# Pairwise message layer and attention: the tail of a batch element rebuilt and moved

## The reference

```python
# layer 0: a message for each pair (i, j)
hi = x @ W1[:H];  hj = x @ W1[H:]
h  = relu(hi[:, :, None, :] + hj[:, None, :, :] + b1)
y  = layernorm(h @ W2 + b2) * gamma + beta       # over the features, for every pair
o  = einsum('bij,bijh->bih', adj, y)
x1 = _layernorm(x + o)
# layer 1: attention
Wh = x1 @ W_w.T + W_b
s  = (Wh @ a_w[:C])[:, :, None] + (Wh @ a_w[C:])[:, None, :] + a_b
e  = exp(s) * adj;  alpha = e / e.sum(axis=2)
out = _layernorm(x1 + alpha @ x1)
```

## Time and profile before

| | |
|---|---|
| median of 3 runs | 2623.7 us (2622.17 to 2623.79) |
| profiled execution, span | 2621.4 us |
| TensorE busy | 2577.0 us, 98% |
| TensorE weight loads | 2049.5 us, 78% |
| VectorE busy | 2337.8 us, 89% |
| ScalarE busy | 2332.6 us, 89% |
| GpSimd busy | 1999.1 us, 76% |
| chain that ended last | PE 58%, DVE 24%, issue 11%, ACT 6% |

### The profile page before, as it was taken

How to read it: one execution, slowest core, us unless ns; L and a number is a source line. 1 busy time by engine, 2 the same in 40 slices (tenths; PEclk the granted TensorE clock), 3 DMA queues, 4 the chain that set the end, 5 groups by cost and what they waited for, 6 DMA issues and landing times.

```text
span 2621.4 us, 77145 instructions
## 1 busy us (share of the span) xinstructions
PE 2577.0 (98%) x21263; PEld 2049.5 (78%) x21263; DVE 2337.8 (89%) x18135; ACT 2332.6 (89%) x3650; POOL 1999.1 (76%) x1163
## 2 busy tenths in 40 slices
PE   8999999999999999999999999999999999999997
PEld 7777777777777777777777777777777777777774
DVE  7889988989899889998898989988988999989897
ACT  7899899899998998989989889999899898998996
POOL 7777777777777777777777777777777777777773
PEclk9999999999999999999999999999999999999999
DMA  0000000000000000000000000000000000000000
GB/s 17 8 12 7 11 7 10 11 6 11 11 6 11 6 11 11 6 11 11 6 11 6 11 11 6 11 10 7 11 6 11 11 6 11 8 8 11 6 7 7
DMA packets 48051, 23.49 MB, mean 9 GB/s; under 512 B 6208, under 2 KB 47808, under 8 KB 47808
## 3 DMA queue, kind: packets, MB, share of 16 engines
q1 hardware_dynamic: 46512, 21.12, 2.9%
q10 hardware_dynamic: 1296, 0.20, 0.0%
HBM read 17.11 MB, written 4.19 MB: 8 GB/s over the span
## 4 chain that ended last, share of the span: by engine, by line
PE 58%; DVE 24%; issue 11%; ACT 6%; POOL 0%; ACTq 0%; DVEq 0%; DMA 0%
PE y_ps L529 42%; DVE squares L517 16%; PE agg_ps L573 12%; DVE q L517 3%; ACT y L263 3%; DVE x1e L488 2%; ACT h L281 1%; ACT L334 1%; PE prep_ps L529 1%; PE tail_ps L529 1%; DVE o_sb L455 1%; PE tail_ps L584 1%; PE att_ps L529 1%; DVE eT L509 0%; DVE si_cols L499 0%
## 5 line engine op out<-in xcount | busy, mean ns | idle before, releaser
L252 POOL TENSOR_TENSOR h<-bT,aT 128x1024 f32<-128x1024 f32 x1024 | 1951.1, 1919 | 584.3 <-PE y_ps L529 572.9
L529 PEld LDWEIGHTS y_ps<-w_pair,h 128*128 128x128 f32 x16384 | 1885.7, 192 | 313.0 <-DVE q L517 260.3
L529 PE MATMUL y_ps<-w_pair,h 128*128 128x128 f32 x16384 | 1991.3, 278 | 21.9 <-DVE q L517 9.3
L517 DVE CUSTOM_DVE_ANT_0 squares<-y_ps,y 128x128 bf16<-128x128 f32 x8192 | 1842.3, 282 | 185.0 <-ACT y L263 171.2
L263 ACT ACTIVATE y<-y_ps 128x508 f32<-128x508 f32 x2048 | 1162.4, 595 | 190.8 <-PE y_ps L529 173.9
L281 ACT ACTIVATE h<-h 128x1024 f32<-128x1024 f32 x1024 | 1085.3, 1060 | 10.2 <-POOL h L252 10.2
L517 DVE DVE_READ_ACCUMULATOR2_ANT q<- 128x1 f32 x8192 | 659.1, 80 | 0.0
L573 PE MATMUL agg_ps<-y,wz 128*32 128x512 f32 x4096 | 545.9, 606 | 1.7 <-DVE o_sb L455 1.7
L573 PEld LDWEIGHTS agg_ps<-y,wz 128*32 128x32 f32 x4096 | 81.1, 108 | 66.7 <-issue 3.1
L492 DVE CUSTOM_DVE_ANT_0 s_terms<-x1e,v1row 128x128 f32<-128x128 f32 x64 | 99.5, 1554 | 0.1
L334 ACT ACT_TABLE_LOAD x64 | 82.1, 1283 | 4.3 <-DVE sj L504 3.2
(11 more groups left out here) (90 smaller groups left out, 740.4 us busy)
## 6 DMA issues: line engine op xcount, KB each, us to landing
x_in<-in_x_dram SPq DMA_DIRECT2D x64, 64.0 KB, 1.8
adj_in<-in_adj_dram SPq DMA_DIRECT2D x64, 64.0 KB, 1.9
x_res<-in_x_dram SPq DMA_DIRECT2D x64, 64.0 KB, 1.8
adj_res<-in_adj_dram SPq DMA_DIRECT2D x64, 64.0 KB, 1.9
out_dram<-x_out SPq DMA_DIRECT2D x64, 64.0 KB, 1.6
w<-in_L_gnn_W_dram ACTq DMA_DIRECT2D x1, 64.0 KB, 2.4
w1a<-in_L_gnn_W_dram SPq DMA_DIRECT2D x1, 64.0 KB, 2.2
w1b<-in_L_gnn_W_dram SPq DMA_DIRECT2D x1, 64.0 KB, 2.3
```

What stands on the lines that cost most here:

```text
L252: nc.gpsimd.tensor_tensor(h[:, u % HRING].rearrange("k (r g) s -> k r g s", g=GROUPS), bT[:, p, :].unsqueeze(1).unsqueeze(1).broadcast_to( ...
L517: last = nc.vector.tensor_tensor_reduce(out=squares[:, k % YRING, n, :], in0=y_ps[k % YRING][:, n, :], in1=y[:, p, i, :], scale=1.0, scala ...
L529: return nc.tensor.matmul(dst, lhsT, rhs, start=start, stop=stop)
```

## The change

- `x1p`, `ex` and `x2p` now lie in the PSUM bank of `att_ps`, `v` in that of `tail_ps`. They were in SBUF.
- rstd and the two layernorm factors are exp(-0.5 ln(var + eps)), both steps on ScalarE, with one table set loaded at the start. Before it was Sqrt on ScalarE and a reciprocal on VectorE, and tables were changed twice a slot.
- The score sums read `x1p` with the factor as their scale, and the rows v1row and v2row are made free of their mean in the set-up. `si_cols` is made by ScalarE, and the residual plus beta by ScalarE (`beta_part`) and GpSimd (`x_beta`, at its unit 7).
- Tail and finish of an element are in one slot, each step one unit behind the one that it needs: o_sb in VectorE's unit 1, its transpose before TensorE's unit 2, oT copy in ScalarE's unit 3, w_back before unit 4, x1p in unit 5, Ln and Exp in 6, x1e and the score sums in 7, si_cols in 8, scores before 9, ex in 10, eT in 11, attention before 12, x2p in 13, Ln and Exp in 14, x_out in 15.
- The eight groups of sums of an element come in four bursts of two, behind units 6, 9, 12 and 15 of one slot.
- `pair_weights` is at GpSimd's unit 5, `prep` a unit earlier on each engine. ScalarE's Ln and Exp of `v` stand in unit 0, ahead of the copy of quart 0 and behind the relu of unit 2. The last slot of the program falls away.

The diff, cut to its core:

```diff
-    WEIGHTS_UNIT = 4
-    POOL_WEIGHTS_UNIT = 8
-    CHUNK_STEP = UNITS // CHUNKS
-    EARLY_CHUNKS = (UNITS - WEIGHTS_UNIT) // CHUNK_STEP
+    POOL_WEIGHTS_UNIT, POOL_RESIDUAL_UNIT = 5, 7
+    BURST = {u: range(c, c + 2) for u, c in ((6, 0), (9, 2), (12, 4), (15, 6))}
...
+        v = tail_ps[:, 2, :]
+        x1p = ex = att_ps[:, 2 * K:3 * K]
+        x2p = att_ps[:, 3 * K:4 * K]
...
             # GpSimd
+                    if tail and u == POOL_RESIDUAL_UNIT:
+                        pool.wait_ge(beta_part_ready, t - 1)
+                        pool.wait_ge(xres_loaded[p], nth16(half, p, -2) * 2)
+                        nc.gpsimd.tensor_tensor(x_beta[:], beta_part[:], x_res[:, p, :], ALU.add).then_inc(x_beta_ready, 1)
...
             # ScalarE, behind the relu of unit u + 2 and ahead of the copies of unit u
+            nc.scalar.preload_act_table_set("natural_log_exp_and_others")
...
-                    if gather and u == 2:
-                        act.wait_ge(v_ready, t)
-                        nc.scalar.activation(sd[:], v[:], ACT.Sqrt, bias=epsc[:, 0:1], scale=1.0 / K).then_inc(sd_ready, 1)
+                    if gather and u == 0:
+                        act.wait_ge(v_ready, t)
+                        nc.scalar.activation(ln_v[:], v, ACT.Ln, bias=epsc[:, 0:1], scale=1.0 / K).then_inc(ln_v_ready, 1)
+                        act.wait_ge(ln_v_ready, t)
...
+                        nc.scalar.activation(rstd[:], ln_v[:], ACT.Exp, scale=-0.5).then_inc(rstd_ready, 1)
+                    if tail and u == 2:
+                        act.wait_ge(adj_sum_ready, t - 1)
...
+                        nc.scalar.activation(beta_part[:], beta_rows[:], ACT.Identity, scale=adj_sum[:, 0:1]).then_inc(beta_part_ready, 1)
+                    if tail and u == 3:
+                        act.wait_ge(oT_ps_s, t - 1)
...
+                        copy(oT_sb[:], tail_ps[:, 0, :]).then_inc(oT_sb_s, 1)
+                    if tail and u == 6:
+                        act.wait_ge(mv1_ready, t - 1)
+                        nc.scalar.activation(ln1[:], mv1[:, 1:2], ACT.Ln, bias=epsc[:, 0:1]).then_inc(ln1_ready, 1)
...
+                    if tail and u == 14:
+                        act.wait_ge(mv2_ready, t - 1)
+                        nc.scalar.activation(ln2[:], mv2[:, 1:2], ACT.Ln, bias=epsc[:, 0:1]).then_inc(ln2_ready, 1)
+                        act.wait_ge(ln2_ready, t - 1)
+                        nc.scalar.activation(rs2[:], ln2[:], ACT.Exp, scale=-0.5).then_inc(rs2_ready, 1)
...
             # VectorE
-                    if gather and (u, e) == (2, 0):
-                        nc.vector.reciprocal(rstd[:], sd[:]).then_inc(rstd_ready, 1)
-                    if tail and (u, e) == (3, 0):
+                    if tail and (u, e) == (0, 1):
+                        dve.wait_ge(xres_loaded[p], nth16(half, p, -2) * 2)
...
+                        nc.vector.reduce_sum(adj_sum[:], adj_res[:, p, :], axis=mybir.AxisListType.X).then_inc(adj_sum_ready, 1)
+                    if tail and (u, e) == (1, 0):
                         dve.wait_ge(agg_done, (t - 1) * CHUNKS)
                         nc.vector.tensor_scalar(o_sb[:], agg_ps[:, 0:K], part[:, 0:1], None, ALU.mult).then_inc(o_part, 1)
-                    if tail and u == 3 and 1 <= e < CHUNK:
+                    if tail and u == 1 and 1 <= e < CHUNK:
...
+                    if tail and (u, e) == (7, 1):
+                        nc.vector.tensor_tensor_reduce(out=s_terms[:, 1, :], in0=x1p, in1=v1row[:], scale=rs1[:, 0:1], scalar=0.0,
+                                                       op0=ALU.mult, op1=ALU.add, accum_out=si[:, 0:1]).then_inc(si_ready, 1)
...
+                    if tail and (u, e) == (15, 0):
+                        dve.wait_ge(rs2_ready, t - 1)
...
             # TensorE
-                    if finish and u == 0:
-                        pe.wait_ge(eT_ready, t - 2)
-                        mm(att_ps[:, 0:K + 1], eT[:], x1e[:]).then_inc(att_done, 1)
-                    if tail and u == 6:
+                    if tail and u == 2:
                         pe.wait_ge(o_stored, t - 1)
+                        if gather:
+                            pe.wait_ge(ln_v_ready, t)
                         nc.tensor.transpose(tail_ps[:, 0, :], o_sb[:], ident[:]).then_inc(oT_ps_s, 1)
-                    if tail and u == 8:
+                    if tail and u == 4:
                         pe.wait_ge(oT_sb_s, t - 1)
                         mm(tail_ps[:, 1, :], oT_sb[:], w_back[:]).then_inc(f_ps_s, 1)
...
+                    if tail and u == 12:
+                        pe.wait_ge(eT_ready, t - 1)
+                        pe.wait_ge(x1_ready, t - 1)
+                        mm(att_ps[:, 0:K + 1], eT[:], x1e[:]).then_inc(att_done, 1)
...
+                    if gather and u in BURST:
+                        for chunk in BURST[u]:
...
+                            weighted_sums(1 - p, chunk)
```

More of the change, by code:

```diff
@@ L107, in gnn_pair_kernel @@
         q = sb("q", [S, 2, S])
-        v, sd = sb("v", [S, S]), sb("sd", [S, S])
+        ln_v = sb("ln_v", [S, S])
         rstd = sb("rstd", [S, S])
@@ L176, in _, with slot @@
                     sp.dma_start(b1c[:], b1.rearrange("(p o) -> p o", o=1)).then_inc(s_w1, 16)
-            def slot(t, half, p, pairs, prep, gather, tail, finish, early):
+            def slot(t, half, p, pairs, prep, gather, tail, early):
                 if pairs and not (isinstance(t, int) and t + 2 >= B):
@@ new lines, in slot @@
+                    if tail and (u, e) == (13, 1):
+                        dve.wait_ge(rz_ready, t - 1)
+                        dve.wait_ge(x1_ready, t - 1)
+                        nc.vector.scalar_tensor_tensor(out=x2p, in0=att_ps[:, 0:K], scalar=rz[:, 0:1], in1=x1e[:, 0:K],
+                                                       op0=ALU.mult, op1=ALU.add).then_inc(x2p_ready, 1)
+                    if tail and (u, e) == (13, 2):
+                        dve.wait_ge(x2p_ready, t - 1)
+                        nc.vector.bn_stats(st2[:], x2p).then_inc(st2_ready, 1)
@@ new lines, in slot @@
+                    if tail and (u, e) == (13, 3):
+                        dve.wait_ge(st2_ready, t - 1)
+                        dve.sem_inc(s_passed, 1)
+                        nc.vector.bn_aggr(mv2[:], st2[:]).then_inc(mv2_ready, 1)
+                    if tail and (u, e) == (15, 0):
+                        dve.wait_ge(rs2_ready, t - 1)
+                        if early >= 3:
+                            dve.wait_ge(stored[1 - p], nth16(half, p, -3))
+                        nc.vector.tensor_scalar(x_out[:], x2p, mv2[:, 0:1], rs2[:, 0:1], ALU.subtract, ALU.mult).then_inc(out_ready, 1)
```

203 lines of the change are left out of this document (76 added, 127 removed).

## The result

The changed kernel takes 2879.8 us (median of 4 runs, 2876.3 to 2883.9) against 2623.1 (2622.2 to 2623.8) of the kernel before, both timed on the same chip: ratio 1.098, 95% interval 1.096 to 1.100. Slower, by 257 us; 2880 had been forecast. The profiled execution spans 2874.2 us (before 2621.4).

The account below looks back on a forecast made before the run. TensorE, busy 98% of 2621.4 us, was taken as the bound. Per slot 40.34 - 0.9 - 1.35 + 3.5 + 0.45 + 1.6 = 43.65; 62 slots add 205, back edges 53, drain -3, median 2.3: say 2880 us, range 2700 to 2960.

Parts of the forecast that it names:

- the PEclk row: Sign expected in the profile after: granted clock below 1.0 behind the wait, and this row showing 8 and 9.
- The added wait: TensorE, at the transpose of o_sb before unit 2, waits for VectorE's last o_sb: 3.5 us a slot taken.
- the walk: Step-by-step timing of TensorE, ScalarE and VectorE from the end of unit 15's matmuls (T) to the last o_sb: wait 3.7 us.
- Rival B: At the transpose ScalarE is prompt, wait 2.6 us, half the back edge hides: 2796 us, about 2700 without clock fall; chance 0.13.
- rival C: Wait at the transpose is at its 1.6 us floor, clock holds, back edges hide: 2593 us; chance 0.05.
- The back edge: At each of 28 loop turns VectorE is held before v; counted whole, 1.9 us each, 53 us in all.
- The other short links: TensorE waits for oT_sb before unit 4 (about 0.2 us) and eT before unit 12 (0.25): +0.45 a slot.
- own work of 38.1: TensorE's work per slot without waits, said to fall from 39.4 to 38.1 us with sums in bursts.
- The clock: TensorE's granted clock falls after the wait at the transpose: 1.6 us charged per slot, bounds 0 and 2.5.
- Rival A: The wait at the transpose is as computed but TensorE's clock holds: 2780 us; chance 0.17.
- saving of -1.35: On TensorE, the second group of a burst costs 0.86 us, not 1.20: -0.34, four times a slot.
- TensorE's 0.9 us of waits: TensorE's waits per slot in the kernel before, all granted as returned by the relief of VectorE and ScalarE: -0.9.

Follow-up runs that it names:

- experiment 1: Changed kernel with TensorE's transpose of o_sb before unit 3 instead of unit 2: 2681.2 us, ratio 1.022.
- Experiment 5: Changed kernel with ScalarE's Ln and Exp of v in unit 2, not 0, and GpSimd's scaled weights one unit later: 2793.1 us, ratio 1.065.
- experiment 11: Changed kernel with tail spread out, Ln and Exp of v in unit 2, bursts behind units 1, 6, 10, 13, o_sb in VectorE's unit 2: 2542.3 us.
- experiment 2: Changed kernel with 14 useless products on TensorE ahead of its wait for o_sb: 2831.1 us, ratio 1.080.
- experiment 7: Changed kernel with about two units between each tail step and its consumer, and Ln and Exp of v in ScalarE's unit 2: 2579.4 us, ratio 0.983.
- experiment 8: Kernel of experiment 7 with its eight groups of sums done singly, not in four joined pairs: 2669.2 us, ratio 1.018.
- experiment 3: Kernel before with only its sums changed, to four bursts of two groups behind units 6, 9, 12 and 15: 2826.1 us, ratio 1.078.
- experiment 12: Kernel of experiment 11 with four slots to a turn of the loop: 2518.9 us, ratio 0.961.
- experiment 10: Kernel before with its sums joined in four pairs behind units 3, 7, 11 and 15: 2641.2 us, ratio 1.007.

## Why the prediction was right

The number came out within 1 us of the median, which is better than its terms: three of them are off by 0.2 to 0.5 us a slot, and they cancel.

**The mechanism.** It was as forecast: the transpose directly behind the matmuls of quart 3 (experiment 1 moves it and takes back 77% of the loss), its wait released by VectorE's o_sb and longer in every second slot. One sign was wrong: the PEclk row read 9 throughout, not 8 and 9.

**The added wait, 3.5 taken, 3.7 by the walk.** It measured 3.32. With T = 1467.74 (start of the last burst) the walk had Ln at T+3.65, the copies of quart 0 at T+4.4, VectorE's first square of it at T+5.05 and the last o_sb ready at T+9.25; the trace has 3.46, 4.08, 4.68 and 8.95. The error is at the front: ScalarE was late, but less than I had it (quart 31 copied at T+1.61, not T+1.9), and Ln and Exp took 0.62 from start to copy, not 0.75. The step said "until ScalarE has copied quart 3 and VectorE has worked up to the last o_sb". Only the second half binds, from quart 0's copy on. Experiment 5 shows that the steps on v ahead of that copy were 0.8 of it. Rival B's 2.6 and rival C's 1.6 did not come.

**The back edge, 1.9 a turn.** The waits differ by 5.34 - 3.32 = 2.0. It hid nowhere, as counted; not counted was that the long wait lets the clock fall each time.

**The other short links, 0.45.** From the transpose at 1388.02 to the end of the last matmul ahead of the next one (1432.31 - 5.22 = 1427.09) are 39.07 us at full clock, where 38.1 + 0.45 were forecast: 0.5 too little. The two links named are there (the w_back product starts 0.27 behind its matmuls at 1392.04, attention 0.24 at 1411.79). The own work of 38.1 is itself good: experiment 11 runs plain slots of 38.31. Beside a plain slot of experiment 11 the sums (7.40 and 7.41) and the small products (1.60 and 1.59) take the same time, start to start, and the whole difference lies in the y products (30.07 and 29.31). What holds it there beyond the two links was not tried.

**The clock, 1.6.** By difference it was 44.57 - 39.07 - 3.32 - 28/59 x 2.02 = 1.2 a slot. The 32 records behind the transposes, summed over the 59 slots, give 1.3. The forecast had one fall in each slot; falls came behind the long waits and behind a third of the short ones. Rival A (the clock holds) is out by these rows and by experiment 2. The loss is spread too thin for the PEclk row of tenths. The Trainium skill, TensorE: Matmul & The Clock Gate (The HAM clock gate), says that an array which has been idle drops to half rate, and these traces agree in direction: 0.66 granted over the stretch with the 5.22 wait, 0.998 over experiment 7, whose longest wait at the y products is 1.3.

**The sum.** v starts at 51.8 and last at 2849.7, so a slot is 44.41 by the measure that gave 40.34 before; forecast were 43.65 and 0.85 of back edges, 44.50. The drain, from the last y matmul on, takes 27.6 (2846.65 to 2874.2) and took 30.0 (2591.4 to 2621.4): -2.4, where -3 was said.

**Where the reasoning was thin.** The saving of -1.35 was booked for the bursts without asking what the sums covered. Its size is right (experiment 8), but in the kernel before the same bursts cost 203 us (experiment 3), part of it through VectorE's meetings with GpSimd. The prediction survived because the wait at the transpose was worked out with the seam already bare. It also granted all of TensorE's 0.9 us of waits to the relief of VectorE and ScalarE. What that relief, 225 and 108 us of busy time, bought in the changed kernel no run isolates. One part can be estimated: v now writes to PSUM and took 0.35 us in all 64 slots, in 29 of them beside GpSimd; had it met GpSimd as in experiment 3, at 1.8, the wait at the transpose, whose chain it is in, would be some 1.4 us longer. Whether the relief carries the gain of experiments 7, 11 and 12 was not tried: experiment 10, which has neither the relief nor late bursts, ends 0.7% above the kernel before, and it differs in more than one thing.

## What to carry to other kernels

Lay a consumer behind at least two units of other work from its producer, on the engine that bounds the kernel: the same operations took 2880, 2681 and 2579 us as the chain was loosened, and one unit more between o_sb and its transpose took 2591 to 2542. Work that looks like overhead on the bounding engine may be what covers another engine's seam, so before joining or moving it ask what that other engine does meanwhile, and place it there. Count a wait on TensorE with the clock that it costs afterwards.

## What the runs showed of the hardware that was not expected

- The length of a wait does not decide alone on a fall of the granted clock. Behind 3.3 us the same matmuls ran at full speed in 21 of 32 slots of one kernel and in 8 of 47 of its version with four slots a turn; behind 2.5 us (experiment 5) in 15 of 34; behind 5.2 us and more they were slow each time (5.2 to 6.5 us for 32 records).
- A VectorE operation from SBUF to SBUF that starts while GpSimd is in one of its 1.9 us operations on h ends just behind that operation. All 120 such v of the kernel before and experiments 3 and 10 ended 0.08 to 0.10 us behind it, all 186 such first score sums 0.15, whatever their length (0.29 to 1.94 us for v); the 72 v that met no operation on h took 0.29. With its output in PSUM v took 0.35 us in all 64 slots of the changed kernel, 29 of them beside GpSimd. So the mean of such an operation (v: 400 ns before, 1779 in experiment 3) is set by when it starts.
- VectorE idles 1.9 to 2.9 us at each back edge of the loop with nothing to wait for (52.9 us in 28 before, 37.2 in 13 in experiment 12). What that costs the kernel depends on what TensorE has at hand: 0.36 us in the kernel before (slots of 40.59 against 40.23), 1.6 between experiments 11 and 12, and 2.0 with a fall of the clock behind it in the changed kernel.
